# Head attention: a unit's value products in one run in the second tile of the next unit, and its copy and split one tile earlier

## The reference

```
qh, kh, vh = heads_split(q @ Wq), heads_split(k @ Wk), heads_split(v @ Wv)
dots = einsum('bhid,bhjd->bhij', qh, kh) * scale
dots = where(mask, -big, dots)            # mask: True where a context row is valid
attn = softmax(dots)
out  = einsum('bhij,bhjd->bhid', attn, vh)
x = x + out.reshape(b, n, h*d) @ Wo + bo
```

## Time and profile before

| | |
|---|---|
| median of 3 runs | 1468.39 us (1465.25 to 1469.49) |
| the profiled execution | 1472.92 us, its span 1471.2 us |
| this stage | from 513 us to about 1001 us of the span |
| PE busy over the span | 1399.7 us (95%) |
| DVE / ACT / POOL busy | 1021.7 / 778.5 / 294.8 us |

### The profile page before, as it was taken

One profiled execution on the slowest core, in us unless ns is written; L12 is line 12 of the kernel. 1 busy time (PEld: TensorE's weight loads), 2 busy tenths in 40 slices (PEclk: granted clock), 3 DMA queues, 4 the chain that ended last, 5 costly groups with the idle time before them and its releaser, 6 DMA issues.

```text
span 1471.2 us, 27431 instructions
## 1 busy us (share of the span) xinstructions
PE 1399.7 (95%) x9946; PEld 1117.6 (76%) x9946; DVE 1021.7 (69%) x2459; ACT 778.5 (53%) x1681; POOL 294.8 (20%) x331
## 2 busy tenths in 40 slices
PE   6899998998999879999999999988999999999998
PEld 5898997885556556666667666657889999999997
DVE  6767773565657668877877787776487766777753
ACT  4556663334766467677877777763442232222221
POOL 0000001242254322300000000023233333233321
PEclk9999999999999989999999999989999999999999
DMA  9432201323555111100000000002036544555431
GB/s 348 138 111 68 82 15 55 119 87 111 172 182 178 43 46 31 37 13 2 16 23 20 13 30 2 2 1 63 1 74 150 131 101 110 129 125 115 103 100 55
DMA packets 78479, 117.80 MB, mean 80 GB/s; under 512 B 7487, under 2 KB 51845, under 8 KB 77829
## 3 DMA queue, kind: packets, MB, share of 16 engines
q1 hardware_dynamic: 75269, 107.59, 26.0%
q0 software_dynamic: 3072, 8.39, 1.8%
HBM read 97.09 MB, written 18.87 MB: 79 GB/s over the span
## 4 chain that ended last, share of the span: by engine, by line
PE 58%; DVE 4%; issue 2%; ACT 1%; DVEq 0%; ACTq 0%
PE PS L68 13%; PE PS L69 13%; PE PS L70 13%; PE PS L2600 6%; PE PS L2573 6%; PE PS L2587 3%; PE PS L2615 3%; DVE c_sm L2809 1%; DVE c_pr L2818 1%; ACT c_pr L2689 1%; PE PS L1895 0%; DVE st L360 0%; DVE c_u L2822 0%; PE PS L388 0%; DVE c_k L2787 0%
## 5 line engine op out<-in xcount | busy, mean ns | idle before, releaser
L1968 ACT ACTIVATE d_hf<-PS,C 128x512 f32<-128x512 f32 x160 | 109.1, 691 | 262.1 <-PE PS L70 260.4
L2698 ACT ACTIVATE c_pt<-PS 100x512 f32<-100x512 f32 x256 | 139.0, 595 | 97.5 <-PE PS L2587 97.4
L953 POOL CAST d_h<-d_hf 128x512 fp32r<-128x512 f32 x160 | 128.1, 813 | 303.9 <-DVE d_hf L2050 248.4
L68 PE MATMUL PS<-d_w,d_h 128*128 128x256 f32 x640 | 182.1, 285 | 1.4 <-issue 1.4
L70 PE MATMUL PS<-d_w,d_h 128*128 128x256 f32 x640 | 179.8, 281 | 0.0
L69 PE MATMUL PS<-d_w,d_h 128*128 128x256 f32 x640 | 179.8, 281 | 0.0
L2689 ACT ACTIVATE c_pr<-c_sm,c_mn 128x400 f32<-128x400 f32 x256 | 158.7, 626 | 20.1 <-DVE c_mn L2809 20.1
L2809 DVE CUSTOM_DVE_ANT_0 c_sm<-PS,c_mw 128x400 f32<-128x400 f32 x256 | 136.2, 570 | 21.3 <-PE PS L2573 17.6
L958 DVE TENSOR_TENSOR d_h<-d_hf,d_h 128x512 fp32r<-128x512 f32 x160 | 131.8, 881 | 13.2 <-POOL d_h L953 13.2
L2050 DVE TENSOR_TENSOR d_hf<-d_hf,d_wb 128x512 f32<-128x512 f32 x128 | 89.8, 709 | 71.0 <-ACT d_hf L1968 70.5
L2573 PEld LDWEIGHTS PS<-c_k,c_q 64*128 64x128 f32 x768 | 63.0, 189 | 85.8 <-issue 49.6
(11 more groups left out here) (304 smaller groups left out, 3139.5 us busy)
## 6 DMA issues: line engine op xcount, KB each, us to landing
d_wb<-wscratch SPq DMA_DIRECT2D x64, 512.0 KB, 7.5
a_cT<-ctxT SPq DMA_DIRECT2D x4, 1601.0 KB, 8.0
a_raw_nat<-ctx SPq DMA_DIRECT2D x4, 1536.0 KB
zs<-e_zero SPq DMA_DIRECT2D x2, 2944.0 KB, 23.0
ys<-e_y SPq DMA_DIRECT2D x46, 128.0 KB, 1.8
d_w1r<-l_w SPq DMA_DIRECT2D x10, 512.0 KB, 4.1
d_w2r<-l_w SPq DMA_DIRECT2D x10, 512.0 KB, 5.2
e_z<-zs SPq DMA_DIRECT2D x9, 512.0 KB, 4.3
```

What stands on the lines that cost most here:

```text
L68: pe.matmul(out, w[0], x[0], start=first, stop=False)
L953: i = eng.tensor_copy(mem["h"][b % 2][0][:, m, :], mem["hf"][:, m, :])
L1968: act.activation(memD["hf"][:, m, :], PS[:, m, :], ACT.Silu, bias=C[:, b1 + g * 4 + m:b1 + g * 4 + m + 1]).then_inc(DM["act"], 1)
L2698: act.activation(c_pt[u % 2][0:KW, :, :, i * P + r * DH:i * P + (r + 1) * DH].rearrange("p h t q -> p (h t) q"), PS[0:KW, BT + r, :].rearr ...
```

## The change

Unit u-1's attend was in two halves, one behind the turn of the second tile and one behind that of the third tile. Now both stand behind the turn of the second tile, and PE has nothing of it in the third. ACT's copy and DVE's split of the attended rows stood at the head of the fourth tile's work and stand now in the third tile's: on ACT ahead of the turned copies, on DVE between normalised and masked. Nothing is added or taken away, and no size changes.

```diff
@@ w_pe
                                 ln_turn(pe, s_ln, b, j, BK, freed=1)
-                        if 1 <= u <= UNITS:
-                            attend(u - 1, i - 1)
+                        if i == 1 and 1 <= u <= UNITS:
+                            attend(u - 1, 0)
+                            attend(u - 1, 1)
                     elif u + 2 < UNITS:
@@ w_act
-                    if i == 3 and u >= 1:
+                    if i == 2 and u >= 1:
                         attended(u - 1)
                     if u < UNITS:
                         turned(s)
@@ w_dve
-                    if i == 3 and 1 <= u <= UNITS:
+                    if i == 2 and 1 <= u <= UNITS:
                         attended(u - 1)
                     if s + 2 < UNITS * QT:
                         masked(s + 2)
```

## The result

The changed kernel took 1497.83 us in the median of 4 runs (1497.26 to 1500.07), the kernel before 1468.44 us beside it (1465.25 to 1469.49). The ratio is 1.0207, with a 95% interval of 1.0188 to 1.0226: 29 us slower, where 31.3 were forecast. The profiled execution of the changed kernel has a span of 1498.3 us, 27.1 more than that of before.

What follows compares the result with a forecast made beforehand. PE's own instruction list was taken to bound each unit. Terms 27.1 + 3.5 + 0.9 + 0 - 0.2 = 31.3 us, added to 1468.4, gave 1499.7 us, range 1486 to 1512.

Steps and rivals of the forecast that it cites:

- The way from scores to scores: Third tile's scores through masks to the fourth's scores: 1.98 us bare, against 1.19 us of PE work without attend.
- 21 plain units, 27.1 us: Fourth tile's scores 1.29 us late in each plain unit, the split delaying the masks; nothing given back later.
- 5 units with layer-norm transposes, 3.5 us: Transposes on PE in the third tile leave 0.60 us of cover, so each unit loses 0.69 us.
- 0.7 us in hand: Slack of the masks for the next unit's start; ACT's 0.6 us delay in layer-norm units uses it up, no more.
- 3 units in which DVE was late, 0.9 us: Split costs 0.60 us ahead of already late masks, the fourth tile wins some back: +0.3 us each.
- u = 30, 0 us: Third tile's masks already late there; the split's 0.60 us only moves from one late mask to the other.
- The end, -0.2 us: Last unit: joining the attend halves wins 0.6 us, the turn's wait for ACT's copy costs 0.4.
- The floor of 0.79 us would hold: With the split hidden, the third tile's PE list still waits 0.79 us per plain unit; 17.5 us in all.
- rival A: The split is hidden and only the bare way counts: +17.5 us, 1486 us; chance 0.10.
- the lower bound: Least loss allowed for the change: 21 x 0.79 + 5 x 0.19 = 17.5 us, if the split were hidden.
- Rival B, the clock: PE's clock falls after the new 1.3 us gaps: 1545 us, or 1510 to 1520 in few units; chance 0.07.
- Rivals C and D: C: busy PE isn't bound, no change, 1468 us, chance 0.03. D: fewer PE waits, faster, 1456 us, chance 0.02.

Runs made afterwards that it cites:

- e6: Changed kernel with values of unit u+3 moved from the first to the third tile in 19 plain units, split still ahead of the masks; ratio 1.0014.
- e5: Kernel before, with attend joined in the second tile, values in the third and split behind the masks, in 19 plain units only; 1467.73 us, ratio 0.998.
- e1: Kernel before, with only the two attend halves joined in the second tile, copy and split left in the fourth; 1518.44 us, ratio 1.0331.
- e3: Changed kernel with the split of the attended rows behind the third tile's masks instead of ahead of them; 1498.39 us, ratio 1.0185.
- e7: e3 with values of unit u+3 moved to the second tile, behind both attend halves, in 19 plain units; ratio 1.0126.
- e2: Kernel before, with only copy and split moved to the third tile, attend halves left in the second and third; 1580.84 us, ratio 1.0743.
- e9: Changed kernel with the split of the attended rows done twice, the second behind the first; ratio 1.0488.

## Why the prediction was right

- **The bound.** TensorE's own list set a unit's length before; e6 and e5 show it from the other side, since with the gap filled the unit is TensorE's list again, 14.15 us.
- **The way from scores to scores.** Worked out as 1.98 us bare; e1, e3 and e7 have 1.98 in their plain units. With the split in it 672.80 - 670.33 = 2.47; the changed kernel has 2.48, in all plain units. With both halves where they were, 5.53; e2 has 5.53.
- **21 plain units, 27.1 us.** Measured 24.5 us (sum of the differences between the two timelines from unit to unit), mostly 1.0 to 1.15 each instead of 1.29. The size was off in one term: two halves in one run are not 2 x 1.87 = 3.74 us but 3.59 (701.25 to 704.84), so joining them saves 0.15 us a unit. I had put that at 0.07 at most.
- **5 units with layer-norm transposes, 3.5 us.** 4.1 us: 0.5 to 0.7 in three, 1.1 in two. The fourth tile is 4.0 us there, not 3.9: the "0.7 us in hand" was used up and a little more. The unit behind such a unit loses 0.4 us more in its first tile (4.60 instead of 4.26).
- **3 units in which DVE was late, 0.9 us.** 0.5 us. The 1.5 us that the term takes from the earlier trace rows were a wait of weight loads; the matmuls of queries waited for the split for only 0.3 us in 2 cases. **u = 30, 0 us.** -0.1 us. What holds DVE up there is the pair of normalising operations, which takes 5.08 us in the kernel before and 5.09 in the changed one instead of 0.77, while two operations of GpSimd on `d_w` run (2.37 and 2.47 us); in e1, e3, e5 and e6 only 2.9 us, and the unit is 2.2 to 2.4 us shorter than before. So this term could have come out otherwise by 2.3 us. **The end, -0.2 us.** 0.5 us more instead of less.
- **The rest of the profiled pair.** The changed kernel's profiled execution won 2.5 us in step u = 0, which the change doesn't touch: its TensorE had full clock from 534 to 542 us, where the one before ran at 0.50 until 540. The medians, which don't hang on one execution, differ by 29.4 us.
- **The step that was wrong without showing.** "The floor of 0.79 us would hold", 17.5 us, if the split were hidden: rival A and the lower bound. e3 hides the split and stays at ratio 1.0185, some 27 us. The split of the keys and the values behind it are a second way round the unit, of 15.36 us. I had looked at the chain of masks only for the fourth tile and the next unit's start, and not followed it to the next engine that waits for DVE. The forecast held because the second way is no longer than the first in the changed kernel, and that was luck: in its unit behind the one shown, the split of the keys ends at 713.19 + 0.56 = 713.75 and values start at 713.90, 0.15 us later, as they do in e3 (702.70 and 702.85), where they count as waiting for it.
- **Rival B, the clock.** Right to leave it at a low chance for this change, with a gap of 1.22 us: the clock stayed at 1.00 from 660 to 720 us. The prediction's row for an idle stretch of this length, 996 to 998 us, has only 0.77 us of idle in it; the timeline has the whole stretch, 1.42 us, from the attend's end at 997.23 to 998.65, and the clock is 1.00 in the 2 us behind it as well. The clock decided e2 and e9. The Trainium skill, "TensorE: Matmul & The Clock Gate", section "A second HAM failure mode: psum-queue depth-cycling", tells of frequent micro-idles that make the clock swing; e9 agrees (15 of 20 plain units, 1.5 us each, at idle stretches of 1.95 us), the changed kernel does not, at 1.22 us.
- **Rivals C and D** fell: TensorE's busy time was a true measure of its bound here, although its weight loads were busy for only 69% of the stretch.

## What to carry to other kernels

Work between two instructions of one engine that are tied through other engines is cover: before moving it, compare the engine's own list between the two with the way through the others, link by link (here 1.19 us against 2.48). Where that way is longer, put other work in, as values here, rather than shorten the way: a shorter way may only meet the next one, as in e3. A dependent operation in front of another in an in-order list hands its wait on, and such hand-overs could be priced here from single rows of the timeline (2.47 us worked out, 2.48 measured); what can't be had so is the second way, so follow each engine's delay once round the whole loop.

## What the runs showed of the hardware

- The clock of TensorE in this loop, by the wait in the third tile: 1.22 us (the changed kernel, in both of its profiled executions) and 1.36 us (six units of e9), no such unit with a slower fourth tile; 1.95 us (e9), 15 of 20 units with a fourth tile of 5.3 to 5.4 us instead of 3.9 (granted clock 0.68 over it); 2.41 us (e2, on another chip than e9), 20 of 29 units with 5.3 to 6.8 us (0.53 over 6.7 us). The loss from a longer wait is 1.5 to 2.9 us on top of the wait.
- Two runs of 8 attend products (64 columns each, two heads side by side) take 1.87 us each, 16 in one run 3.59 us. So a second boundary between such a group and its neighbours costs 0.15 us.
- The same values products take 1.54 us behind project in the first tile (678.13 to 679.67 in the kernel before) and 1.56 us behind the turn in the third (737.19 to 738.75 in e5).
- VectorE's two normalising operations (128x400 each) take 0.77 us together, and 5.08 us while two GpSimd operations over 128x1024 run beside them (u = 30 of the kernel before, 969.00 to 974.08).
